# A graph network in four layers: three sums of tiles, and one chunk's norms and mean, at other places in the order of steps

## The chip, the cores and the metric

The kernel runs on one core of a Trainium2 chip. The time is device microseconds of one execution, as the median of three runs. Its engines are TensorE (PE in the profile), VectorE (DVE), ScalarE (ACT), GpSimd (POOL) and SyncE (SP, which issues the DMAs here). Each works through its own queue in order; between them semaphores tell that a step is done.

## The reference

`x` is (8, 2048, 64), `adj` a sparse (2048, 2048) matrix whose rows sum to one. Four layers follow each other, each `x = layernorm(x + L(x, adj))`:

```python
# L0: per-node weights from an embedding of 16, terms 1, A, 2AA-1 of x
w = jnp.einsum('nd,dkio->nkio', embedding, weight)
out = jnp.einsum('bnki,nkio->bno', x_g, w) + b
# L1: attention over edges above 0.5, then elu
# L2: agg = (adj + 1) @ (x W^T + b) / degree
# L3: three steps of effects = adj @ v; h = relu([v, effects] W1 + b1); v = h W2 + b2
```

With these inputs every row of `adj` has two or more entries, so none is above 0.5, and the kernel computes L1 as one mean over all nodes, and checks by flags that it may (a slow general path stands behind a branch and isn't taken).

## The kernel before

The 512 columns (8 batches of 64) are four chunks `c` of 128; the 2048 nodes are 16 tiles of 128, grouped in four quarters `j`. All engines run through the same lists of steps: `HEAD` (lines 87 to 95), `MIDDLE` from `middle_order()` (line 98 on) and `TAIL` from `last_order()`. A step is a tuple, and each engine does its own part of it, in the order of the list. So a list is the order of every engine's queue.

`MIDDLE` holds layer 0's 64 rounds, `Z` with `add`: round 4u + t, with unit u = 4c + j, is one tile of one chunk. PE multiplies the tile's three terms with the 16 embedding weights: two halves g of 18 matmuls each, into three pairs of PSUM banks in turn. VectorE adds five of the eight results of each half into `X` and `Y`, ScalarE copies three scaled into `AT`, and GpSimd (`add`) sums these into `AC` and then all into `X`: five operations, one of 384 columns and four of 128. ScalarE's part of a round waits (`s_ab`) until GpSimd's first operation of the round before has read `AT`; PE's half waits (`s_za`) until ScalarE has read the half three before it.

Ahead of a round's `Z` stand a quarter or two of the products for later units (`P2`, `P1`, bank 0, evicted by `E2`, `E1`: high half on ScalarE, low half on VectorE), and in units with c < 3 and j < 2, so in rounds 0 to 7, 16 to 23 and 32 to 39, a term: `dx` or `t1` in bank 1, evicted by ScalarE, VectorE and, for `t1`, GpSimd (a split into high and low half).

`at(g, steps)` puts steps behind round g. `xs` k (`dve_xs`, `pool_xs`) takes the sums of tiles 2k and 2k+1 over the 64 channels on VectorE, and subtracts the mean and adds the bias on GpSimd, with four operations of 512 columns. A round of chunk 0 needs this for its tile (`s_xc`), and `E1 12` needs it for tiles 0 to 7, `E1 14` and `scales 1` for all 16. `scales` are small steps on VectorE, one on ScalarE.

The norm of layer L and chunk c is `sq` (square, ScalarE) and `red` (sum, VectorE) for each quarter, `var` (VectorE, with a root on ScalarE), `rs` (five small VectorE steps) and an `apply` for each quarter (VectorE). Behind layer 0's norm stand `sum` (three adds on GpSimd), `mean` (PE), `row_a` and `row_b` (VectorE, with an exp on ScalarE) and `addrow` for each quarter (GpSimd); behind layer 1's the `split` for each quarter: high half on ScalarE, low half and a bias add (`bc`) on GpSimd. `bt` are 64 GpSimd steps that build combined masks for later; `chk` is a count on ScalarE. For chunk c these begin at round 16(c+1) + 3: chunk 0 in rounds 19 to 37, chunk 1 in 35 to 53, chunk 2 in 51 to 69; chunk 3 has an order of its own behind round 63. What is put at rounds 64 and later stands in `TAIL`, among the products `P` of layer 2 (evicted by `E`), the steps `W` and `D`, and the checks `ovr` and `sgn`.

Of the kernel before, what the change touches and what calls it, by code (L numbers as in the profile page):

```python
# [58 lines left out]
def pieces(kind, n):  # L59
    return [(kind, n, q) for q in range(4)]  # L60
# [22 lines left out]
def place(p, c, j):  # L83
# [7 lines left out]
        + pieces("P1", 0) + [("E1", 4), ("E1", 5), ("wm",), ("E1", 6), ("E1", 7), ("E1", 8)]  # L91
        + pieces("P1", 1) + [("nb",), ("wn",), ("E1", 9), ("dx", 0), ("t1", 0), ("dx", 1), ("t1", 1), ("dx", 2)]
        + [("xs", 0)]
        + pieces("P1", 2) + [("t1", 2), ("dx", 3), ("t1", 3), ("xs", 1), ("E1", 10), ("bounds",), ("xs", 2)]
        + pieces("P1", 3)[0:3] + pieces("P2", 0) + [("E2", 0), ("P1", 3, 3), ("E1", 11)])


def middle_order():

    after, rest = {}, {}

    def at(g, *steps):

        (after if g < 64 else rest).setdefault(g if g < 64 else g - 64, []).extend(steps)

    for c in range(NC):
        g = 16 * c
        for j in range(4):  # L110
            late = (c, j) == (3, 3)
            at(g + 4 * j + (4 if late else 6), ("sq", 0, c, j))
            at(g + 4 * j + (4 if late else 7), ("red", 0, c, j))
        g += 16
        if c < 3:
            at(g + 3, ("var", 0, c))
            at(g + 4, ("rs", 0, c), ("apply", 0, c, 0))
            for j in (1, 2, 3):
                at(g + 4 + j, ("apply", 0, c, j))
            at(g + 7, ("sum", c))  # L120

            g += 9
            at(g, ("mean", c), ("row_a", c))
            at(g + 1, ("row_b", c))
            for j in range(4):
                at(g + 2 + j, ("addrow", c, j))
                at(g + 4 + j, ("sq", 1, c, j))
                at(g + 5 + j, ("red", 1, c, j))
            at(g + 8, ("var", 1, c))
            for j in range(4):  # L130
                at(g + 9 + j, *[("rs", 1, c)][j:], ("apply", 1, c, j), ("split", c, j))
        else:
            at(g, ("var", 0, c), ("rs", 0, c), *[("apply", 0, c, j) for j in range(4)], ("sum", c))
            at(g + 5, ("mean", c), ("row_a", c), ("row_b", c))
            for j in range(4):
                at(g + 6, ("addrow", c, j))
            for j in range(4):
                at(g + 6 + j // 2 / 2, ("sq", 1, c, j))
                at(g + 6.5 + j // 2 / 2, ("red", 1, c, j))
            at(g + 7, ("var", 1, c))  # L140
            for j in range(4):
                at(g + 8 + j, *[("rs", 1, c)][j:], ("apply", 1, c, j), ("split", c, j))

        for k in range(4):
            at(16 * c + 9 + 2 * k, ("chk", 4 * c + k))
    for k in range(5):
        at(2 * k + 1, ("xs", 3 + k))
    at(9, ("scales", 0))
    at(11, ("scales", 1))
    at(13, ("scales", 2))  # L150
    at(15, ("scales", 3))
    for k, g in enumerate((18, 24, 27, 29)):
        at(g, ("scales", 4 + k))

    free = [2, 4, 6, 8] + [g for g in range(10, 64) if g not in (23, 39, 55) and g % 16 not in (2, 3, 4, 5)]
    free = sorted(free + [g for g in (18, 19, 20, 21, 56, 57, 58, 60, 61, 62)][:48 - len(free)])
    for i in range(48):
        at(free[i], ("bt", i))
    order = []
    for u in range(16):  # L160
        c, j = divmod(u, 4)
        beside = []
        if u in (1, 2, 5, 6):
            v = {1: 4, 2: 5, 5: 6, 6: 7}[u]
            beside += pieces("P1", v) + [("E1", 8 + v)]
        beside += pieces("P2", u + 1) + [("E2", u + 1)] if u < 15 else pieces("P", 0) + [("E", 0)]
        each = len([x for x in beside if x[0][0] == "P"]) // 4
        for t in range(4):
            n = 0
            while beside and (n < each or beside[0][0][0] == "E"):  # L170
                n += beside[0][0][0] == "P"
                order.append(beside.pop(0))
            order += [("Z", u, t), ("add", u, t)]
            order += after.pop(4 * u + t, [])
            if c < 3 and j < 2:
                v = 4 * (c + 1) + 2 * j + t // 2
                order.append(("dx" if t % 2 == 0 else "t1", v))
    return order, rest
# [119 lines left out]
def cut(n, jj, what):  # L298
    return "cut", n, jj, what

MIDDLE, _rest = middle_order()
TAIL = last_order(_rest)
_cut = TAIL.index(("branch",))
# [1969 lines left out]
```

How the kernel before makes its waits and increments, by code:

```python
    def __call__(self, ins):  # L42
        ins.then_inc(self.sem, 1)
        self.n += 1
        self.e.wait_ge(self.sem, self.n)
# [669 lines left out]
        def sync_head(e):  # L715
# [4 lines left out]
            def pair(m):  # L720
                if m >= RING:
                    e.wait_ge(s_bm, 2 * (m - RING) + 2)
                h, t = divmod(2 * m, NT)
                e.dma_start(landing[m % RING].rearrange("p (t i) -> p t i", t=2),
                            atr[:, h, t:t + 2, :]).then_inc(s_ring[m % RING], 16)
# [11 lines left out]
            e.dma_start(SM[:, :], sm_in).then_inc(s_small, 16)  # L738
            e.dma_start(BX, bx_in.rearrange("p (k n) -> p k n", n=128)).then_inc(s_bx, 16)
            tiles_of_x(4)
            pair(4)
            pair(5)
            for h in range(2):
                e.dma_start(T3[64 * h:64 * h + D, 0:1024 + C], embt_in[D * h:D * h + D, :]).then_inc(s_embed, 16)
            tiles_of_x(5)
            for m in range(6, NT):
                pair(m)
            e.wait_ge(s_zp, 8 * NT)
            for it in range(NT):
                if it:
                    e.wait_ge(s_sign, it)
                e.dma_start(rowt, ar[it]).then_inc(s_land, 16)
# [1 line left out]
        def sync_fast(e):  # L754
            for u, (c, j) in enumerate(x[1:] for x in TAIL if x[0] == "out"):
                e.wait_ge(s_n[3], u + 1)
                e.dma_start(orr[:, c, 4 * j:4 * j + 4, :], xpart(c, j)).then_inc(s_out, 16)
            e.wait_ge(s_out, 16 * 16)
# [2 lines left out]
        def pe_aux(e, step):  # L761
            e.wait_ge(*aux_free[step])
            return bank(aux_bank[step])
```

## Time and profile before

| | us |
|---|---|
| median of 3 runs | 1032.59 (1032.51 to 1033.38) |
| profiled execution | 1033.26 |
| its span | 1031.5 |
| PE busy | 1008.9 |
| DVE busy | 678.2 |
| POOL busy | 555.2 |
| ACT busy | 456.5 |

The span goes from the first instruction to the last; about 1.8 us lie around it. The granted TensorE clock was 0.996 of full speed on the mean. The 64 rounds lie between 108.13 and 525.22 us. Times within the trace count from the start of the span. A mark in square brackets behind a row tells how long the engine was idle before it and who ended that; a row without one followed its engine's previous work directly, or nearly so.

### The profile page before, as it was taken

The numbers are of one execution on the slowest core, as the hardware profiler recorded it, in microseconds if no ns is written. First come the engines' busy times: TensorE is split into PE (matmuls) and PEld (weight loads), VectorE is DVE, ScalarE is ACT, GpSimd is POOL, SyncE is SP. The second block draws the span as 40 slices with busy tenths as digits, with TensorE's granted clock in tenths as the row PEclk, the third lists the DMA queues.
The fourth block names the chain that finished last, engine by engine and source line by source line (L and its number), as shares of the span: only waits on it lengthen the run. The fifth ranks groups of instructions, "written<-read, shape, count | busy, mean of one in ns | idle before, by whom it ended". The sixth has DMA issues, their size and how long they took to land.

```text
span 1031.5 us, 18649 instructions
## 1 busy us (share of the span) xinstructions
PE 1008.9 (98%) x6854; PEld 485.1 (47%) x6854; DVE 678.2 (66%) x1683; ACT 456.5 (44%) x1109; POOL 555.2 (54%) x645
## 2 busy tenths in 40 slices
PE   7999999999999999999999999999999999999995
PEld 3445444444444444434445556555555545455552
DVE  3886565656577796577667767786763546657556
ACT  4632233453345545543552554342556555232632
POOL 0004498666558698879878465474534243323311
PEclk9999999999999999999999999999999999999998
DMA  9930000000000000000010111000032231000022
GB/s 367 403 141 1 1 2 2 1 2 1 1 1 2 1 2 2 1 2 1 1 42 1 41 42 42 2 1 1 2 123 98 107 123 42 3 2 21 21 62 62
DMA packets 14658, 45.65 MB, mean 44 GB/s; under 512 B 960, under 2 KB 9280, under 8 KB 10080
## 3 DMA queue, kind: packets, MB, share of 16 engines
q1 hardware_dynamic: 14560, 44.39, 11.8%
q8 instruction: 56, 0.92, 0.4%
q14 instruction: 42, 0.34, 0.1%
HBM read 40.19 MB, written 4.19 MB: 43 GB/s over the span
## 4 chain that ended last, share of the span: by engine, by line
PE 83%; DVE 9%; ACT 3%; DMA 2%; issue 1%; POOL 0%; SPq 0%; ACTq 0%; DVEq 0%; POOLq 0%
PE PS L961 28%; PE PS L924 23%; PE PS L794 21%; DMA BW<-at_in 2%; PE PS L779 2%; PE PS L781 2%; PE PS L780 2%; DVE BW L1227 1%; DVE T L1230 1%; ACT WZ L1074 1%; DVE X L1230 1%; DVE X L1542 1%; PE PS L788 1%; PE PS L787 1%; PE PS L786 1%
## 5 line engine op out<-in xcount | busy, mean ns | idle before, releaser
L794 PE MATMUL PS<-BW,S 128*128 128x512 fp8e4 x1280 | 290.9, 379 | 1.2 <-DVE R L1230 0.7
L1074 ACT ACTIVATE T<-PS,SM 128x128 f32<-128x128 f32 x384 | 113.1, 366 | 208.5 <-DVE X L1230 127.3
L924 PE MATMUL PS<-WZ,R 64*128 64x512 f16 x1536 | 198.0, 377 | 1.7 <-ACT T L1074 1.7
L794 PEld LDWEIGHTS PS<-BW,S 128*128 128x128 f16 x1280 | 120.2, 98 | 150.1 <-issue 17.0
L961 PE MATMUL PS<-BW,S 128*128 128x512 fp8e4 x768 | 173.1, 379 | 0.0
L1748 POOL TENSOR_TENSOR T<-T 128x128 f32<-128x128 f32 (+1 forms) x192 | 125.0, 651 | 73.0 <-ACT T L1074 62.9
L1230 DVE SCALAR_TENSOR_TENSOR X<-PS,SM,X 128x128 f32<-128x128 f32 x320 | 109.6, 342 | 77.8 <-PE PS L924 76.9
L924 PEld LDWEIGHTS PS<-WZ,R 64*128 64x128 f16 x1536 | 69.5, 94 | 104.6 <-issue 26.3
L961 PEld LDWEIGHTS PS<-BW,S 128*128 128x128 f16 x768 | 73.8, 98 | 83.3 <-issue 0.5
L961 PE MATMUL PS<-BW,T 128*128 128x512 fp8e4 x480 | 109.3, 379 | 0.0
L1748 POOL TENSOR_TENSOR S<-R,S 128x512 f16<-128x512 f32 (+1 forms) x46 | 52.7, 1153 | 102.4 <-ACT S L1074 102.4
L1230 DVE SCALAR_TENSOR_TENSOR T<-PS,SM,T 128x128 f32<-128x128 f32 x256 | 87.8, 343 | 27.5 <-PE PS L924 27.5
L924 PE MATMUL PS<-WZ,T 64*128 64x512 f16 x768 | 103.8, 376 | 0.0
L1748 POOL TENSOR_TENSOR T<-R,T 128x512 f16<-128x512 f32 x40 | 50.6, 1273 | 85.0 <-ACT T L1074 51.3
L1074 ACT ACTIVATE WZ<-WZ,ra 128x2048 f16<-128x2048 f32 (+1 forms) x32 | 63.8, 1994 | 41.2 <-DMA WZ<-a_in 41.2
L1230 DVE SCALAR_TENSOR_TENSOR R<-PS,cs,R 128x512 f32<-128x512 f32 x48 | 35.9, 749 | 65.7 <-PE PS L788 29.0
L1772 POOL TENSOR_TENSOR BW<-BW 128x512 fp8e4<-128x512 fp8e4 x64 | 70.8, 1112 | 2.7
L961 PEld LDWEIGHTS PS<-BW,T 128*128 128x128 f16 x480 | 46.3, 98 | 52.9
L1230 DVE SCALAR_TENSOR_TENSOR R<-PS,ra,R 128x128 f32<-128x128 f32 x176 | 48.6, 341 | 31.0 <-PE PS L781 17.8
L1748 POOL TENSOR_TENSOR X<-X,T 128x128 f32<-128x128 f32 x128 | 59.3, 463 | 10.0
L779 PE MATMUL PS<-hat,T 128*128 128x128 f16 x320 | 57.2, 219 | 3.4 <-DVE T L1230 2.5
L846 PE MATMUL PS<-BW,S 128*128 128x512 fp8e4 x240 | 53.6, 386 | 6.1 <-DVE BW L1227 6.1
(210 smaller groups left out, 1494.6 us busy)
## 6 DMA issues: line engine op xcount, KB each, us to landing
WZ<-a_in SPq DMA_DIRECT2D x16, 1024.0 KB, 4.8
BW<-at_in SPq DMA_DIRECT2D x8, 1024.0 KB, 19.1
R<-at_in SPq DMA_DIRECT2D x7, 1024.0 KB, 13.8
out<-X SPq DMA_DIRECT2D x16, 256.0 KB, 2.3
X<-x_in SPq DMA_DIRECT2D x3, 1024.0 KB, 21.1
T<-w_in SPq DMA_DIRECT2D x1, 1536.0 KB, 16.6
R<-at_in SPq DMA_DIRECT2D x2, 512.0 KB, 4.5
SM<-sm_in SPq DMA_DIRECT2D x1, 520.5 KB, 19.2
```

The lines of the kernel that those rows point to most:

```text
L779: e.matmul(ok, th, hat[:, 0, kind, :], start=True, stop=False)
L780: e.matmul(ok, tl, hat[:, 0, kind, :], start=False, stop=False)
L781: m = e.matmul(ok, th, hat[:, 1, kind, :], start=False, stop=True)
L786: e.matmul(o, hat[:, 0, kd, :], T[:, c, 0, block(j)], start=alone, stop=False, skip_group_check=on)
L794: m = e.matmul(o, stile(h, t, c), Bm[:, t, block(j)], start=(t == 0 and h == 0), stop=(last and t == NT - 1 and h == 1))
L846: e.matmul(bank(2 * c + j), stile(h, jt, c), Bm[:, jt, block(j)], start=(jt == 0 and h == 0), stop=False)
L924: m = e.matmul(bank(b0 + q), halves[kd][zh][r, :], WZ[r, wh, kd, block(g)], start=(i == 0), stop=(i == 8))
L961: m = e.matmul(o, half_of(n, what, h, q % 2)[:, t, :], b[:, 4 * (q % 2) + t, :], start=(s in (0, 1, 3) and q % 2 == 0 and t == 0 and h == ...
L1074: return e.activation(o, i, f, **kw)
L1230: return e.scalar_tensor_tensor(out=o, in0=a, scalar=s, in1=b, op0=f, op1=g)
L1748: return e.tensor_tensor(o, a, b, f)
L1772: e.tensor_tensor(o, a, b, f, saturate=False).then_inc(s_bt, 1)
```

## The change

Three things move; no step is added or removed. `xs 2` goes from the end of the head to behind round 1, and `xs 3` to `xs 7` two rounds further on each, to rounds 3 to 11. `scales 0` to `scales 4` follow by two rounds. And for chunk 1 everything that is counted from `g` (the norm of layer 0, `sum`, `mean`, the row steps, the norm of layer 1, the splits) goes six rounds further on: to rounds 41 to 59 in place of 35 to 53. The squares and sums of layer 0's own norm stay where they are, as do the `bt` and `chk` steps.

```diff
--- before.py
+++ after.py
@@ -91,7 +91,7 @@
         + pieces("P1", 0) + [("E1", 4), ("E1", 5), ("wm",), ("E1", 6), ("E1", 7), ("E1", 8)]
         + pieces("P1", 1) + [("nb",), ("wn",), ("E1", 9), ("dx", 0), ("t1", 0), ("dx", 1), ("t1", 1), ("dx", 2)]
         + [("xs", 0)]
-        + pieces("P1", 2) + [("t1", 2), ("dx", 3), ("t1", 3), ("xs", 1), ("E1", 10), ("bounds",), ("xs", 2)]
+        + pieces("P1", 2) + [("t1", 2), ("dx", 3), ("t1", 3), ("xs", 1), ("E1", 10), ("bounds",)]
         + pieces("P1", 3)[0:3] + pieces("P2", 0) + [("E2", 0), ("P1", 3, 3), ("E1", 11)])
 
 
@@ -111,7 +111,8 @@
             late = (c, j) == (3, 3)
             at(g + 4 * j + (4 if late else 6), ("sq", 0, c, j))
             at(g + 4 * j + (4 if late else 7), ("red", 0, c, j))
-        g += 16
+
+        g += 22 if c == 1 else 16
         if c < 3:
             at(g + 3, ("var", 0, c))
             at(g + 4, ("rs", 0, c), ("apply", 0, c, 0))
@@ -143,13 +144,14 @@
 
         for k in range(4):
             at(16 * c + 9 + 2 * k, ("chk", 4 * c + k))
-    for k in range(5):
-        at(2 * k + 1, ("xs", 3 + k))
-    at(9, ("scales", 0))
-    at(11, ("scales", 1))
-    at(13, ("scales", 2))
-    at(15, ("scales", 3))
-    for k, g in enumerate((18, 24, 27, 29)):
+
+    for k in range(6):
+        at(2 * k + 1, ("xs", 2 + k))
+    at(11, ("scales", 0))
+    at(13, ("scales", 1))
+    at(15, ("scales", 2))
+    at(17, ("scales", 3))
+    for k, g in enumerate((20, 24, 27, 29)):
         at(g, ("scales", 4 + k))
 
     free = [2, 4, 6, 8] + [g for g in range(10, 64) if g not in (23, 39, 55) and g % 16 not in (2, 3, 4, 5)]
```

## Rows read from the trace of the kernel before

**Rows 1.** The page, section 1: busy us (share of the span), xinstructions of each engine.
```profile
PE 1008.9 (98%) x6854; PEld 485.1 (47%) x6854; DVE 678.2 (66%) x1683; ACT 456.5 (44%) x1109; POOL 555.2 (54%) x645
```

**Rows 2.** Waits: engine, line it waits at <- who ended it: us in total, times, longest.
```profile
PE PS L924 <- ACT T L1074: 1.7, 1, 1.7
...
PE PS L832 <- DVE R L1230: 1.6, 2, 1.3
```

**Rows 3.** Timeline of PE, 113 to 130: start us, us, engine, line, out<-in [idle before].
```profile
114.40 0.82 PE L924 MATMUL PS<-WZ,R 64*128 64x512 f16 x6
...
120.67 0.82 PE L924 MATMUL PS<-WZ,R 64*128 64x512 f16 x6
...
124.47 0.82 PE L924 MATMUL PS<-WZ,R 64*128 64x512 f16 x6 [1.69 <-ACT T L1074]
...
128.80 0.82 PE L924 MATMUL PS<-WZ,R 64*128 64x512 f16 x6
```

**Rows 4.** Timeline of POOL, 104 to 126.
```profile
117.83 1.03 POOL L1720 TENSOR_TENSOR X<-X,hat 128x512 f32<-128x512 f32 x1 [7.38 <-issue]
...
122.51 2.06 POOL L1748 TENSOR_TENSOR T<-T 128x384 f32<-128x384 f32 x3
```

**Rows 5.** Timeline of PE, 350 to 379.
```profile
363.90 0.82 PE L924 MATMUL PS<-WZ,R 64*128 64x512 f16 x6
...
369.28 0.23 PE L832 MATMUL PS<-i,T 128*128 128x128 f16 x1 [1.32 <-DVE R L1230]
...
371.56 0.82 PE L924 MATMUL PS<-WZ,R 64*128 64x512 f16 x6
```

**Rows 6.** Timeline of DVE, 362 to 369 and 447 to 460.
```profile
364.60 0.88 DVE L1529 TENSOR_TENSOR T<-T 128x32 f32<-128x32 f32 x1
...
449.06 0.19 DVE L1529 TENSOR_TENSOR T<-T 128x32 f32<-128x32 f32 x1
...
456.32 0.68 DVE L1542 TENSOR_TENSOR X<-X,T 128x512 f32<-128x512 f32 x1
```

**Rows 7.** Timeline of PE, 447 to 468.
```profile
449.11 0.82 PE L924 MATMUL PS<-WZ,R 64*128 64x512 f16 x6
...
455.71 0.82 PE L924 MATMUL PS<-WZ,R 64*128 64x512 f16 x6
...
461.53 0.82 PE L924 MATMUL PS<-WZ,R 64*128 64x512 f16 x6
```

**Rows 8.** Groups by form, POOL, 453.3 to 477: xcount, busy us, mean ns, idle us before.
```profile
L1748 POOL TENSOR_TENSOR X<-X,bc 128x512 f32<-128x512 f32 x4 | 5.8, 1440 | 0.3
L1748 POOL TENSOR_TENSOR S<-X,S 128x512 f16<-128x512 f32 x4 | 4.6, 1156 | 0.3
L1748 POOL TENSOR_TENSOR T<-T 128x384 f32<-128x384 f32 x4 | 4.4, 1110 | 1.6 <-ACT T L1074 1.6
L1748 POOL TENSOR_TENSOR T<-T 128x128 f32<-128x128 f32 x6 | 3.3, 556 | 0.5
```

**Rows 9.** Groups by form, POOL, 482.9 to 530.86.
```profile
L1748 POOL TENSOR_TENSOR T<-T 128x384 f32<-128x384 f32 x8 | 8.0, 998 | 3.1 <-ACT T L1074 3.1
...
L1748 POOL TENSOR_TENSOR T<-T 128x128 f32<-128x128 f32 x17 | 7.7, 455 | 1.3
...
L1748 POOL TENSOR_TENSOR X<-X,ROW 128x512 f32<-128x512 f32 x4 | 5.1, 1270 | 0.3
```

**Rows 10.** Timeline of POOL, 440 to 490.
```profile
446.14 0.99 POOL L1748 TENSOR_TENSOR X<-X,T 128x128 f32<-128x128 f32 x2
...
483.45 0.99 POOL L1748 TENSOR_TENSOR X<-X,T 128x128 f32<-128x128 f32 x2
```

**Rows 11.** Timeline of ACT, 518 to 612, and of PE, 600 to 612.
```profile
530.88 0.63 ACT L1074 ACTIVATE R<-X 128x512 f32<-128x512 f32 x1 [0.32 <-POOL X L1748]
...
548.09 0.60 ACT L1074 ACTIVATE T<-PS 128x512 f16<-128x512 f32 x1 [1.12 <-PE PS L944]
...
608.46 0.23 PE L779 MATMUL PS<-hat,T 128*128 128x128 f16 x1 [0.87 <-DVE X L1230]
```

## The prediction

> **What bounds the kernel now.** I read the page first: TensorE is busy 98% of the span [rows 1]. So a change of order can win only where TensorE stands, or lose where it makes TensorE stand. The waits of PE come next. The longest inside the rounds are [rows 2]: one of 1.7 us for ScalarE, and two, 1.6 us together, for a term's low half on VectorE. I count rounds from 0 to 63 (the steps `Z`). The starts of the rounds on PE give the price of each stall, since a round between stalls takes the same time whenever it holds the same matmuls.
>
> Rounds 1 and 2 hold the same kind of work, but round 1 takes 120.67 - 114.40 = 6.27 us and round 2 takes 128.80 - 120.67 = 8.13 us [rows 3]: 1.86 us lost. In the middle of round 2 PE waits for ScalarE [rows 3]. ScalarE was late because it may not overwrite `AT` before GpSimd's first add of round 0, and GpSimd began that add only at 122.51, when the four operations of `xs 2`, begun at 117.83, were through [rows 4]: 4.68 us of queue.
>
> Round 37 takes 371.56 - 363.90 = 7.66 us, 1.39 us over 6.27, and PE waits there for VectorE's low half of `dx 14` [rows 5]. Ahead of it VectorE had `rs` and `apply` of layer 0, chunk 1. A small step of such an `rs` took 0.88 us there, against 0.19 elsewhere [rows 6].
>
> Round 51 takes 6.60 us where the next takes 5.82 [rows 7]: 0.78 us. PE wanted the bank of product `P2 13`, whose low half stood on VectorE behind `rs` and `apply` of layer 1, chunk 1. After round 63 PE stands next at 608.46, for 0.87 us [rows 11], and then hardly before the end.
>
> **The change, part by part.** No instruction is added or removed; only places in the queues change.
>
> Part 1, `xs 2` behind round 1 and the later sums one turn later. GpSimd's first add of round 0 comes to stand at 117.83 in place of 122.51 [rows 4], 4.68 us earlier. That is more than the 1.86 us by which PE was held, so the stall goes: -1.86 us. What is late next is the data: round 4 needs `xs 2`, and ScalarE's `E1 12` ahead of round 5 needs tiles 0 to 7, so `xs 3`. GpSimd does adds 0 and 1, `xs 2`, a split of `t1`, add 2, `bt 0`, add 3 and then `xs 3`. With four adds of some 3.2 us (a first operation of 1.0 and four of 0.46 by [rows 9], with the gaps between them), two `xs` of 4.68 and two steps of about 1.2 us (as the splits of [rows 8]) that is 117.83 + 24.6 = 142.4, if it never waits. PE, freed of its stall, begins round 3 at 120.67 + 6.27 = 126.9 and ends the product of `E1 12` two rounds later, at 139.5 at the earliest. So the eviction may come up to 2.9 us late; but PE asks for its bank only behind the terms of round 5, and I cost it at nothing. The moved `scales` steps are small VectorE steps in rounds that have no stall: nothing.
>
> Part 2, chunk 1's layer-0 norm from rounds 35 to 38 into rounds 41 to 44. `rs` and `apply` leave the queue ahead of `dx 14`. Even unblocked (five steps at the 0.19 us and an apply at the 0.68 of [rows 6]) they are 1.6 us, more than 1.39: -1.39 us. In rounds 41 to 44 no `dx` or `t1` follows. `E2 11` follows `rs` there, as `E2 13` did in round 51, but without a `split` on ScalarE between them; so its high half is done while VectorE still works on the norm, and I cost this at nothing. The wait of 0.3 us at round 35 (chunk 0's norm, the smaller of the two of [rows 2]) is untouched.
>
> Part 3, chunk 1's layer-1 norm and its splits from rounds 50 to 53 into rounds 56 to 59. The stall at round 51 goes: -0.78 us. Sum of the three: -4.03 us.
>
> What it costs lies on GpSimd. The four splits and the bias adds behind them took 4.6 + 5.8 = 10.4 us [rows 8]. They now stand between rounds 56 and 59, where GpSimd also has chunk 2's sum, the `bt` steps and the adds. The room there is little: from the end of add 55 to that of add 63 GpSimd waited 3.1 us in all [rows 9]. There is one credit: GpSimd was then still paying for the splits. Add 55 ended at 484.44, 11.27 us behind the start of its round (461.53 + 2 x 5.82), while a settled one, add 49, ended at 447.13, 9.66 us behind its own (449.11 - 2 x 5.82) [rows 7, 10]. With the splits gone from ahead of it, add 55 is settled: 1.6 us. VectorE's norms slow GpSimd's adds besides. In the stretch of the splits a first add took 1110 ns [rows 8] against 998, and the small ones 556 against 455 [rows 9]: 4 x 0.11 + 6 x 0.10, and as much as the latter again for the second pair, 1.7 us. That stretch held the norms of both chunks; half of it moves, 0.8 us. So the last add of round 63 ends 10.4 + 0.8 - 3.1 - 1.6 = 6.5 us later than now, measured against a PE that never waits.
>
> Who waits for that? ScalarE's square of chunk 3's last quarter starts on that very add [rows 11], and behind it in order stand the reduce, `var`, root, `rs`, four applies, `rs` of chunk 2 and the evictions of the products `P`. The first place where this string has room is 548.09: ScalarE had idled 1.12 us for PE [rows 11]. The chain of waits goes from there through VectorE, ScalarE and GpSimd without a piece of PE until 608.46, where PE waits [rows 11]. So of the 6.5 us PE pays 6.5 - 1.1 = 5.4. A part of it (1 to 2.5 us) will be paid near rounds 61 and 62, where ScalarE waits for GpSimd's add as in round 2; the rest at the latest near 608. Both are the same debt and are not added.
>
> Sum: -4.03 + 5.4 = +1.4 us. The profiled execution was 1033.26 us (span 1031.5) and gives 1034.7; the median of the runs, 0.67 us lower, gives 1034.0 us. Bounds: with no slowdown at all (a bias add at the 1.27 us that [rows 9] has for the same shape: 9.7 for 10.4) the debt is 3.9 and the result 1032.5. With the whole 1.7 us and 0.5 us for VectorE's small steps, it is +2.7: 1035.3.
>
> A rule is to be weighed here. The slowdown of [rows 8] is 0.1 us on most operations, and 0.88 for 0.19 us on VectorE's side [rows 6]. The Trainium skill, "SBUF — State Buffer", section "Who interferes with whom", says that a VectorE instruction with two SBUF inputs and a GpSimd one that reads SBUF exclude each other for the whole instruction. By that rule four applies of 0.68 us each would hold GpSimd for up to 2.8 us in place of my 0.8, and the sum would be +3.4; the rows of GpSimd show less.
>
> **The rivals.**
>
> A. The debt is not passed on: rows 61 to 63 or the string behind them have room that I don't see, and only the gain is left. It gives 1032.59 - 4.03 = 1028.6 us; half of it passed on gives about 1031.3. For it: GpSimd is only 54% busy overall [rows 1], and a new order may fill waits that I counted once. Against it: the last square starts on the add with no room, and the chain behind it shows no PE.
>
> B. Slower. GpSimd and VectorE, both now without pauses in rounds 56 to 59, hold each other up operation by operation. If the four moved applies and the five steps of `rs` cost GpSimd their full length (4 x 0.7 and a little), the debt is 8.4 and the time 1032.59 - 4.03 + 7.4 = 1036.0 us. It decides once the slowdown is above about 1.5 us in place of 0.8; then the result is over the bound of 0.2%.
>
> C. Part 1 doesn't do what it says: `xs 3` comes late for `E1 12`, or the wait only shifts by a round. Then 1.86 us stay: 1035.9 us.
>
> **How the numbers follow.** 0.2% of 1032.6 is 2.1 us, about what a measurement of this kernel can tell from no change: below 1030.5 is faster, above 1034.7 slower. Forecast (debt passed on, 1032.5 to 1035.3, likeliest 1034.0): 0.50, of which 0.14 is above 1034.7. A: 0.32, of which 0.24 is below 1030.5 and 0.08 between. B: 0.13, C: 0.05, both slower. So faster 0.24, within 0.2% 0.44, slower 0.32. The range has to take in A's full gain below and B above, since to leave either out would leave out too much: 1028.6 to 1036.0. The forecast's own range is 1032.5 to 1035.3.
>
> **What would show it.** In the changed kernel's waits of PE the 1.7 us for ScalarE near 124 and the two of 1.3 and 0.7 us near 369 and 454 should be gone; round 2 should take 6.27, rounds 37 and 51 6.27 and 5.82. New: GpSimd without an idle mark from round 56 to 63, a wait of PE for ScalarE near round 61 or 62, and the wait at the end of the chain, 0.87 us now, grown by some 3 us. If that wait is still 0.9 us and no new one stands near round 62, A is right. If GpSimd's adds in rounds 57 to 60 take over 4 us each, B is. I am wrong altogether if PE waits in rounds 42 to 45 for `E2 11` behind the moved norm.

## The result and the profile after

The changed kernel took 1035.1 us (median, 1034.6 to 1036.0) against 1032.9 us (1031.7 to 1034.4) for the kernel before in the same sessions. The ratio is 1.0022, with a 95% interval of 1.0015 to 1.0029. It is slower by 2.2 us: 1.1 us more than the 1034.0 I gave, inside the forecast's own range (1032.5 to 1035.3) near its upper end. The ratio is just over the 0.2% that I had set between "no change" and "slower", and its interval holds that bound.

The page of the changed kernel, section 1 (engine, busy us, share of the span), under its span of 1033.8 us; [rows 1] answer to it:

```profile
PE 1010.2 (98%) x6854; PEld 485.4 (47%) x6854; DVE 675.4 (65%) x1683; ACT 456.3 (44%) x1109; POOL 553.5 (54%) x645
```

It tells nothing: PE is 98% busy in both, and the number of instructions is the same. The waits of PE between 110 and 615 us do tell it (line it waits at <- who ended it: us in total, times, longest). The code behind the change has moved down by two lines, so L926 is what L924 was:

```profile
PE PS L926 <- ACT T L1076: 3.1, 3, 1.9
PE PS L781 <- DVE X L1232: 1.7, 1, 1.7
...
PE PS L834 <- DVE R L1232: 0.3, 1, 0.3
```

Of [rows 2] only the 0.3 us at L834 is left; the other waits are new or grown. They stand in two places. PE's timeline, 495 to 525 and 595 to 612 us (start, us, what, idle before in brackets): the lines with an idle mark, and between them the starts of rounds 60, 61, 62 and 63:

```profile
499.09 0.82 PE L926 MATMUL PS<-WZ,R 64*128 64x512 f16 x6
...
501.63 0.82 PE L926 MATMUL PS<-WZ,R 64*128 64x512 f16 x6 [0.42 <-ACT T L1076]
...
505.51 0.82 PE L926 MATMUL PS<-WZ,R 64*128 64x512 f16 x6
...
508.34 0.82 PE L926 MATMUL PS<-WZ,R 64*128 64x512 f16 x6 [0.71 <-ACT T L1076]
...
512.22 0.82 PE L926 MATMUL PS<-WZ,R 64*128 64x512 f16 x6
...
516.27 0.82 PE L926 MATMUL PS<-WZ,R 64*128 64x512 f16 x6 [1.93 <-ACT T L1076]
...
520.60 0.82 PE L926 MATMUL PS<-WZ,R 64*128 64x512 f16 x6
...
598.57 0.22 PE L781 MATMUL PS<-hat,T 128*128 128x128 f16 x1 [1.36 <-issue]
...
603.64 0.22 PE L771 MATMUL PS<-dg,S 128*128 128x128 f16 x1 [0.34 <-POOL S L1750]
...
610.71 0.23 PE L781 MATMUL PS<-hat,T 128*128 128x128 f16 x1 [1.67 <-DVE X L1232]
```

The first three waits lie in rounds 60, 61 and 62. These rounds take 6.42, 6.71 and 8.38 us, which is 0.60, 0.89 and 2.11 more than the 5.82 of an ordinary round and the 6.27 that round 62 took before (it holds a few matmuls more), 3.60 us in all. The last three waits answer to the single 0.87 of [rows 11]: 3.37 us by their marks, 2.50 more. By the starts it is 2.8 us: from the start of round 63 to the last of these waits it now takes 610.71 - 520.60 = 90.11 us, against 608.46 - 521.16 = 87.30 before. The marks show less because neighbouring rows of PE overlap: a row of six matmuls lasts 0.81 us, but the next one starts 0.65 us behind its start when nothing holds it. The overlap of 0.16 is gone wherever PE waits, and the mark counts only from the end of the row before. So PE pays 3.6 + 2.8 = 6.4 us.

And what was gained. PE's timeline, 113 to 130 us, the starts of rounds 1 to 3, then 360 to 372, the starts of rounds 37 and 38, then 443 to 458, those of rounds 51 and 52:

```profile
114.28 0.82 PE L926 MATMUL PS<-WZ,R 64*128 64x512 f16 x6
...
120.55 0.82 PE L926 MATMUL PS<-WZ,R 64*128 64x512 f16 x6
...
126.82 0.82 PE L926 MATMUL PS<-WZ,R 64*128 64x512 f16 x6
...
361.92 0.82 PE L926 MATMUL PS<-WZ,R 64*128 64x512 f16 x6
...
368.19 0.82 PE L926 MATMUL PS<-WZ,R 64*128 64x512 f16 x6
...
445.73 0.82 PE L926 MATMUL PS<-WZ,R 64*128 64x512 f16 x6
...
451.56 0.82 PE L926 MATMUL PS<-WZ,R 64*128 64x512 f16 x6
```

Rounds 1 and 2 take 6.27 us each, round 37 takes 368.19 - 361.92 = 6.27 and round 51 takes 451.56 - 445.73 = 5.83: all three stalls are gone, 1.86 + 1.39 + 0.78 = 4.03 us, as [rows 3, 5, 7] had them. 6.4 - 4.0 = +2.4 us; round 0 began 0.12 us earlier than in the trace of before, which leaves 2.3. That is what the last of the waits has moved by (610.71 against 608.46), and what the span grew by (1033.8 - 1031.5). The median grew by 2.2.

The debt itself, on GpSimd's timeline, 515 to 535 us, the add of round 63:

```profile
532.89 0.98 POOL L1750 TENSOR_TENSOR X<-X,T 128x128 f32<-128x128 f32 x2
```

No row of GpSimd carries an idle mark from 477.9 us to here. The last add ends at 533.87, where before it ended at 530.85 (the square of [rows 11] begins 0.03 us behind that). It is 3.0 us later although 4.03 us of stalls ahead of it are gone and round 0 began 0.12 us earlier: 7.2 us of debt against a PE that never waits. I had said 6.5. Of these 7.2 us PE pays 6.4, so 0.8 are absorbed on the way, where I had said 1.1.

### The profile page after: what moved, and what is told of

It reads as the page before. It is cut to its first block, busy times and chain, and to the rows that moved or that the text cites. A ratio compares the mean times of both kernels' runs of the same rounds, so it can differ in the third digit from the quotient of the medians.

```text
span 1033.8 us, 18652 instructions
## 1 busy us (share of the span) xinstructions
PE 1010.2 (98%) x6854; PEld 485.4 (47%) x6854; DVE 675.4 (65%) x1683; ACT 456.3 (44%) x1109; POOL 553.5 (54%) x645
## 4 chain that ended last, share of the span: by engine, by line
PE 85%; DVE 6%; POOL 4%; ACT 3%; issue 2%; DMA 0%; POOLq 0%; SPq 0%; ACTq 0%; DVEq 0%
PE PS L963 28%; PE PS L926 22%; PE PS L796 19%; PE PS L848 5%; PE PS L781 2%; POOL X L1750 1%; PE PS L783 1%; PE PS L782 1%; DVE X L1544 1%; POOL T L1750 1%; ACT WZ L1076 1%; PE PS L790 1%; PE PS L789 1%; PE PS L788 1%; DVE X L1232 1%
## 5 line engine op out<-in xcount | busy, mean ns | idle before, releaser
L926 PE MATMUL PS<-WZ,R 64*128 64x512 f16 x1536 | 198.3, 377 | 3.1 <-ACT T L1076 3.1
L926 PEld LDWEIGHTS PS<-WZ,R 64*128 64x128 f16 x1536 | 69.3, 94 | 106.5 <-issue 26.3
L1750 POOL TENSOR_TENSOR S<-R,S 128x512 f16<-128x512 f32 (+1 forms) x46 | 52.9, 1157 | 102.3 <-ACT S L1076 102.3
L926 PE MATMUL PS<-WZ,T 64*128 64x512 f16 x768 | 103.8, 376 | 0.0
```

What stands on the lines that cost most here:

```text
L926: m = e.matmul(bank(b0 + q), halves[kd][zh][r, :], WZ[r, wh, kd, block(g)], start=(i == 0), stop=(i == 8))
L1750: return e.tensor_tensor(o, a, b, f)
```

## The experiments

All ratios are to the kernel before, run on the same chip beside them.

### Each part alone

Part 1 alone, on the kernel before (`scales` two rounds later too, as in the change):

```diff
-        ... ("xs", 1), ("E1", 10), ("bounds",), ("xs", 2)]
+        ... ("xs", 1), ("E1", 10), ("bounds",)]
-    for k in range(5):
-        at(2 * k + 1, ("xs", 3 + k))
+    for k in range(6):
+        at(2 * k + 1, ("xs", 2 + k))
```

> The kernel before with part 1 alone: xs 2 behind round 1, xs 3 to xs 7 and scales 0 to 4 two rounds on; chunk 1 stays where it was. Theory: the wait of PE for ScalarE near 124 us (1.7) goes and nothing comes in its place, the rest of the trace is that of before moved up; span 1.9 us shorter, ratio about 0.9982. Rival (the sum of the tiles comes late and the stall only moves): ratio 1.000, with a wait of PE or of VectorE for GpSimd's X between rounds 3 and 6.

Measured: 1031.21 us, ratio 0.9984 (0.9975 to 0.9993). The waits of PE, 110 to 615 us:

```profile
PE PS L832 <- DVE R L1230: 1.6, 2, 1.3
PE PS L779 <- DVE X L1230: 0.9, 1, 0.9
PE PS L794 <- DVE R L1230: 0.7, 1, 0.7
```

The wait for ScalarE is gone and nothing has come in its place: part 1 is a gain by itself, 1.8 us of the 1.86. Rival C is out.

Parts 2 and 3 alone:

```diff
-        g += 16
+        g += 22 if c == 1 else 16
```

> The kernel before with parts 2 and 3 alone: chunk 1's norms, mean and splits six rounds on; xs and scales stay where they were. Theory: the stalls at rounds 37 and 51 go (-2.2 us), GpSimd's debt is that of the changed kernel and costs some 6.2 us, so +4 us, ratio about 1.004; the wait for ScalarE near 124 us is there, and new ones of some 3.5 us stand at rounds 60 to 62. Rival (the loss of the changed kernel comes from part 1, or from both together): ratio near 1.000 or below.

Measured: 1037.15 us, ratio 1.0041 (1.0027 to 1.0055). The waits of PE, 110 to 615 us:

```profile
PE PS L924 <- ACT T L1074: 4.9, 4, 1.9
...
```

Behind it stand 1.7, 1.4, 0.3 and 0.3. These are the waits of the changed kernel, one by one, with the wait of 1.75 us at round 2 besides, since part 1 is missing here. So the whole loss comes from the moved norm. By the starts it costs 6.4 us and brings 1.39 + 0.78 = 2.2, so +4.2; measured are +4.1. The change is the sum of a part that gains and one that loses.

### A late last add: is GpSimd's lateness handed on?

```diff
+                    if n4 == 63:
+                        for _ in range(5):
+                            pc(add(AC, AC, AC))
```

> The kernel before, where GpSimd does five more operations of 384 columns (each an addition of AC to itself, overwritten at once) ahead of the add of round 63: some 5.3 us more on its queue, of which 0.7 us lies in an idle time; nothing waits for it but the add. It measures what a late last add costs. Theory: the add ends 4.6 us later, the first 1.1 us are covered at ScalarE's eviction near 548, the rest (3.5 us) comes out in PE's waits between 596 and 610 us: ratio about 1.0034. Rival A (the string behind round 63 has room for it): ratio 1.000.

Measured: 1035.79 us, ratio 1.0026 (1.0016 to 1.0037). The kernel before has nothing else changed here. The last add ends at 534.20, 3.35 us later than before, and the rounds ahead of it lie 0.36 us earlier in this trace (the add of round 62 begins at 521.07, before at 521.43): it is 3.7 us late. PE's timeline, 590 to 612 us:

```profile
598.83 0.22 PE L779 MATMUL PS<-hat,T 128*128 128x128 f16 x1 [1.41 <-issue]
...
610.96 0.23 PE L779 MATMUL PS<-hat,T 128*128 128x128 f16 x1 [1.66 <-DVE X L1230]
```

With 0.34 us at 603.90 the three waits are those of the changed kernel to within 0.05 us. The last of them ends 610.96 - 608.46 = 2.50 us later than before, and with the 0.36 us by which the rounds lie earlier 2.9 of the 3.7 us are handed on and 0.8 are absorbed, as in the changed kernel. Most of it is absorbed where [rows 11] show the slack of 1.12 us: in the changed kernel ScalarE's row of 530.88 comes 3.0 us later, its row of 550.13 comes 2.0 us later. Between there and 560.54 the lateness grows again, to 2.2 us; what gives back these 0.2 us I didn't settle. I had expected 4.6 us of lateness and not 3.7. The 0.74 us that GpSimd waited ahead of this add were already taken off in that number; the five operations were shorter than I took them for: the eight rows of 384 and 128 columns take 6.58 us where three took 2.07, so some 0.9 us each and not 1.06.

Rival A falls with this run: the chain has no further room. The same shows across the runs. Wherever the last add comes late, PE's last wait ends 76.8 us behind the end of that add: 76.84 us in the changed kernel, 76.76 here, and 76.79 to 76.80 in the run with four masks moved and in the three runs on the apply below. What makes the last add later makes the whole kernel later.

### The masks out of the way: is it the fullness of GpSimd's queue?

Four `bt` of rounds 56 to 59 (one of the two at round 56 stays) and the one of round 45, put at rounds 39 and 50 to 53:

```diff
-    free = ... if g not in (23, 39, 55) and g % 16 not in (2, 3, 4, 5)]
+    free = ... if g not in (23, 45, 55, 56, 57, 58, 59) and (g % 16 not in (2, 3, 4, 5) or g in (50, 51, 52, 53))]
```

> The changed kernel with only the four mask steps of GpSimd (bt) at rounds 56 to 59 taken out and put at rounds 39 and 50 to 52 instead; the other later ones stay, none goes behind round 63. Theory of the debt on GpSimd (in the changed kernel PE pays some 6 us of GpSimd's lateness: 3.6 at rounds 60 to 62 and 2.5 near 609): a bt takes about 1.1 to 1.2 us, so four of them take 4.4 to 4.8 us off the queue; PE gets back 4 us of the 6.1 (the slack ahead of 548 us takes the rest), so about 1031.0 us where the kernel before has 1032.9, a ratio near 0.998. Rival 1 (the masks only fill what would be waiting time, so that moving them is worth nothing): 1035, 1.002. Rival 2 (the earlier rounds have no room for them and PE waits there instead): 1033 to 1035, with new waits of PE between 435 and 470 us.

Measured: 1030.94 us, ratio 0.9978 (0.9968 to 0.9988), 4.2 us below the changed kernel. The waits of PE for ScalarE at L926 are gone; what is left is 0.3 us at round 35, 0.5 us for VectorE in round 59 and 0.2 + 0.3 + 1.7 from 593 to 605.

The `bt` of rounds 60 to 63 out as well, on top of the last edit, and put behind round 63. Of rounds 56 to 63 only round 56 still has one, not none as the expectation says:

```diff
-    for i in range(48):
+    for i in range(44):
...
-    for i in range(48, 64):
-        at(i - 46, ("bt", i))
+    for i in range(44, 64):
+        at(i - 42, ("bt", i))
```

> The changed kernel, with no bt step between rounds 56 and 63: four go to rounds 39 and 50 to 53, where chunk 1's steps stood, four behind round 63. GpSimd's queue is 8.7 us shorter from round 56 to 63. Theory (the loss is GpSimd's debt of 7.2 us): the debt is gone, PE waits neither at rounds 60 to 62 nor more than 0.9 us near 608, and the whole gain is left: about 4 us below before, ratio 0.996. Rival (the loss is VectorE's, whose norms of chunk 1 and chunk 2 now meet between rounds 52 and 59): ratio near 1.002 as with the change.

Measured: 1030.2 us, ratio 0.9974 (0.9964 to 0.9984). GpSimd again waits for ScalarE ahead of the last add (0.57 us), so its debt is paid by then, also with the one mask at round 56. The time is only 0.7 us better than with four moved, since a wait of 1.62 us near 605 stayed. The next run has no mask from round 55 to 63 and none more behind round 63 than the kernel before. It puts a second one at rounds 42, 43, 44, 48 and 53 (the loops over 48 and 16 masks are again those of the changed kernel):

```diff
+    free = sorted([g for g in free if g < 56] + [18, 19, 20, 21, 42, 43, 44, 53, 48])
```

> The changed kernel with all mask steps of GpSimd out of rounds 55 to 63, as in the run that took them out before, but the surplus stands at earlier rounds (a second one at 42, 43, 44, 48 and 53) and none behind round 63. In the run with four of them behind round 63 PE still waited 1.62 us at 605.6 where the kernel before has 0.87. Theory 1 (these four stood ahead of chunk 3's norms and were paid there): the wait goes back to 0.9 us, the waits of rounds 60 to 62 stay away, one of about 0.5 us in round 59 stays: about 1029.4 against 1032.9, a ratio near 0.9965. Theory 2 (the 0.75 us come from elsewhere in the moved norm, from VectorE's queue): 1030.2, 0.9974, with the wait near 605 at 1.6 us again. If the rounds 42 to 53 have no room, PE waits there for ScalarE behind GpSimd: over 1031.

Measured: 1029.17 us, ratio 0.9958 (0.9944 to 0.9971). The wait near 605 is 1.04 us: 0.58 of the 0.75 us too much are gone. I put this down to the four masks behind round 63. The one of round 56 moved too, but GpSimd's idle time ahead of the last add had covered that one. The last run moves chunk 2's `row_b` one round on as well:

```diff
-            at(g + 1, ("row_b", c))
+            at(g + (2 if c == 2 else 1), ("row_b", c))
```

> As the run with all masks out of rounds 55 to 63 and the surplus at earlier rounds, and besides chunk 2's row_b (VectorE, ahead of its layer-1 norm) one round later, behind round 59 in place of 58. In round 59 PE waited 0.53 us for the bank of E2 15, whose low half stood on VectorE behind that row_b and an apply of chunk 1. Theory (that low half was late because of this queue): with row_b behind it the wait goes, round 59 takes 5.9 us, and the time is 0.5 us below the other run: about 1028.9, a ratio near 0.996. Rival (the apply alone makes it late, or chunk 2's norms, pushed back a round, come late for something behind round 63): no gain, or the wait at the chain's end near 605 grows by as much.

Measured: 1028.62 us, ratio 0.9953 (0.9940 to 0.9967). All waits of PE between 110 and 615 us:

```profile
PE PS L781 <- DVE X L1232: 0.9, 1, 0.9
PE PS L834 <- DVE R L1232: 0.3, 1, 0.3
```

The debt is gone and the 4.03 us are left: 4.2 us below the kernel before. The wait for the low half in round 59 went with `row_b`; the difference in time between these last two runs, 0.5 us, is no more than their intervals, and only the row of the wait shows that it is gone. So the same move of the norm is a gain where GpSimd's queue has room for it, and this version beats both kernels.

### What an apply costs GpSimd

Three runs change only the four applies of layer 1, chunk 1 (rounds 57 to 60 on VectorE). First on 8 columns in place of 512:

```diff
+                    if (L, c) == (1, 1):
+                        v, r = v[:, :, :, 0:1], r.unsqueeze(3)
+                        e.tensor_tensor(v, v, r, ALU.mult).then_inc(s_n[L], 1)
+                        continue
```

> The changed kernel with the four applies of layer 1's norm of chunk 1 (on VectorE, rounds 57 to 60, some 0.7 us each) done on one channel of 64 alone, so all but one channel of that normalization is left out; every step, wait and place stays. It asks what VectorE's applies cost GpSimd. Theory (they share the memory's ports for a part, a few tenths of a us on an operation): the two splits and adds beside them get 0.2 to 0.3 us shorter each, PE gets back 0.5 to 1.2 us: about 1034.2, a ratio near 1.001 against 1.0022 of the changed kernel. Rival (each holds the other for its whole length): 4 x 0.7 = 2.8 us come back, about 1032.3, a ratio below 1.0. Rival 2 (no effect of the applies at all; the small steps of rs and the sums are what slows GpSimd): same 1.0022.

Measured: 1033.32 us, ratio 1.0001 (0.9992 to 1.0010), 1.8 us less than the changed kernel by the medians: more than the theory's 0.5 to 1.2, less than the rival's 2.8. Since the intervals are some 1 us wide on either side, the trace is the surer measure: from the end of add 55 to that of the last add GpSimd takes 53.02 us, against 54.96 in the changed kernel, 1.9 us less. This is where my small slowdown fell. Then a reduce over the same 512 columns, with one operand in SBUF, of the same length:

```diff
+                    if (L, c) == (1, 1):
+                        red(e, r, v, ALU.max).then_inc(s_n[L], 1)
+                        continue
```

> The changed kernel with each of the four applies of layer 1's norm of chunk 1 (VectorE, two operands in SBUF, 512 columns, 0.68 us) replaced by a maximum over the channels of the same 512 columns: one operand in SBUF, about the same length on VectorE. The normalization of that chunk is left out so. With the applies shrunk to 8 columns, GpSimd's operations beside them got 2.1 us shorter in sum and the time fell from 1035.1 to 1033.3. This run tells what does it. Theory (it is the apply's second SBUF operand: each of the two engines waits for the other's whole instruction): the reduces hold up nobody; GpSimd's first operations of rounds 57 to 59 take 2.1 us for three in place of 2.6 to 2.9, and the time is that of the small applies, about 1033.2, a ratio of 1.000. Rival (any VectorE instruction of that length slows GpSimd, whatever its operands): as the changed kernel, 1035.1, 1.002.

Measured: 1033.27 us, ratio 1.0005 (0.9996 to 1.0014). The rows show why. The changed kernel, GpSimd's timeline and VectorE's, 478 to 503 us (the rows of rounds 57 to 59 that bear on it):

```profile
482.96 2.61 POOL L1750 TENSOR_TENSOR T<-T 128x384 f32<-128x384 f32 x3
...
486.71 1.15 POOL L1750 TENSOR_TENSOR S<-X,S 128x512 f16<-128x512 f32 x1
487.94 1.59 POOL L1750 TENSOR_TENSOR X<-X,bc 128x512 f32<-128x512 f32 x1
...
491.61 2.89 POOL L1750 TENSOR_TENSOR T<-T 128x384 f32<-128x384 f32 x3
...
495.64 1.16 POOL L1750 TENSOR_TENSOR S<-X,S 128x512 f16<-128x512 f32 x1
...
499.15 2.56 POOL L1750 TENSOR_TENSOR T<-T 128x384 f32<-128x384 f32 x3
...
481.90 1.13 DVE L1225 TENSOR_SCALAR T<-T 128x32 f32<-128x32 f32 x1
483.07 0.93 DVE L1538 TENSOR_TENSOR T<-T 128x32 f32<-128x32 f32 x1
484.03 0.69 DVE L1544 TENSOR_TENSOR X<-X,T 128x512 f32<-128x512 f32 x1
...
487.23 1.19 DVE L1544 TENSOR_TENSOR X<-X,T 128x512 f32<-128x512 f32 x1
...
495.92 0.69 DVE L1232 SCALAR_TENSOR_TENSOR R<-PS,R 128x512 f16<-128x512 f32 x1 [0.28 <-ACT R L1056]
```

With the reduces, the same stretch and engines:

```profile
482.75 2.06 POOL L1753 TENSOR_TENSOR T<-T 128x384 f32<-128x384 f32 x3
...
487.19 1.27 POOL L1753 TENSOR_TENSOR X<-X,bc 128x512 f32<-128x512 f32 x1
...
490.52 2.07 POOL L1753 TENSOR_TENSOR T<-T 128x384 f32<-128x384 f32 x3
...
497.42 2.06 POOL L1753 TENSOR_TENSOR T<-T 128x384 f32<-128x384 f32 x3
...
483.82 0.69 DVE L1235 TENSOR_REDUCE T<-X 128x8 f32<-128x512 f32 x1
...
487.01 0.67 DVE L1235 TENSOR_REDUCE T<-X 128x8 f32<-128x512 f32 x1
```

The first three operations of an add take 2.06 us together, and with an apply beside them 2.61, 2.89 and 2.56; the bias add takes 1.59 in place of 1.27. Together 0.55 + 0.82 + 0.50 + 0.32 = 2.2 us. About 0.2 of them are not the applies': with the reduces, and with the small applies too, the last two operations of the same add take 1.15 us in place of 0.99, beside a small step of VectorE that here falls into the 2.89. So four applies cost 2.0 us, and from the end of add 55 to that of the last add the run with the reduces takes 53.02 us, 1.9 us less than the changed kernel.

The reduces are as long as the applies (0.69, 0.67), the first two lie beside the same operations of GpSimd, and these take their usual 2.06 and 1.27. So it is not VectorE being busy. A reduce differs from an apply in two things, though: it has one operand in SBUF where the apply has two, and it writes 8 columns where the apply writes 512. The row at 495.92 speaks against the writing: 0.69 us, 512 columns written, with one input from PSUM and one from SBUF, beside a split of GpSimd that takes its usual 1.16. So it is the second operand in SBUF, and each apply holds GpSimd for 0.3 to 0.7 us, up to its whole length of 0.68. The apply at 487.23 shows the other side: it began under the split, which ended at 487.86, and took 1.19 us; I read it as having waited for that end. This agrees with the Trainium skill, "SBUF — State Buffer", "Who interferes with whom": a VectorE instruction with two SBUF inputs and a GpSimd one that reads SBUF exclude each other for the whole instruction, and a `tensor_reduce` never contends on this chip.

The third doubles the request:

```diff
+                    if (L, c) == (1, 1):
+                        fc(e.tensor_tensor(v, v, v, ALU.max))
```

> The changed kernel with one more VectorE instruction ahead of each of these four applies: a maximum of the quarter with itself, 512 columns, both operands in SBUF, 0.68 us, which changes no value. It doubles what a two-operand instruction asks of the port beside a GpSimd queue that never idles. Theory (exclusion for the whole instruction, and GpSimd's lateness is handed on to PE one for one): 4 x 0.5 to 0.7 us more on GpSimd's operations, so 2.0 to 2.8 us more of PE's waits, about 1037.4, a ratio of 1.0042 to 1.005. Rival (the slowdown is a sharing that spreads thin, or the first apply's 0.5 us were an accident of where it fell): under 1 us more, 1.0022 to 1.003. It also adds 4 x 0.7 us on VectorE; if PE then waits for a low half on VectorE near rounds 57 to 60 (as it did for 0.5 us at round 59 with the masks out), that part is no work of the port and is to be read off apart.

Measured: 1036.71 us, ratio 1.0035 (1.0022 to 1.0049), 1.6 us more than the changed kernel, under the 2.0 to 2.8 of the theory. GpSimd's timeline from 489 us to the last add, a row of VectorE, and one of PE:

```profile
489.48 3.05 POOL L1776 TENSOR_TENSOR BW<-BW 128x512 fp8e4<-128x512 fp8e4 x2
...
507.32 2.51 POOL L1752 TENSOR_TENSOR T<-T 128x384 f32<-128x384 f32 x3
...
534.30 0.98 POOL L1752 TENSOR_TENSOR X<-X,T 128x128 f32<-128x128 f32 x2
...
497.42 1.64 DVE L1546 TENSOR_TENSOR X<-X,T 128x512 f32<-128x512 f32 x1
...
502.42 3.31 PE L796 MATMUL PS<-BW,S 128*128 128x512 fp8e4 x8 [3.67 <-DVE R L1232]
```

Two mask steps together grew from 2.15 to 3.05 us, two single ones from 1.09 to 1.54 and 1.55, and further operations by 0.2 to 0.45 each; the last pair of applies comes only at 504.87, so the add at 507.32 is still slowed (2.51 for 2.06). From the end of add 55 to that of the last add GpSimd takes 56.16 us, 1.2 more than the changed kernel's 54.96 and 3.1 more than with no applies of that size. The last add ends at 535.28, 1.4 us later than in the changed kernel (0.2 of it lay ahead of this stretch already); PE's last wait ends at 612.08, also 1.4 us later. So the longer time is GpSimd's lateness, handed on one for one, as the theory had it.

What the theory had wrong is the size: the second request cost GpSimd 1.2 us and not 2.0 to 2.8. The rest fell on VectorE: its eight instructions of 0.68 us took from 0.83 to 1.64. Its queue then ran late, and PE stood 3.67 us in round 59 for a low half. But this wait is no further loss. In its place the three waits of rounds 60 to 62 are gone but for one of 1.02 us in round 59, and so are those of 1.36 and 0.34 us near 598 and 603. PE's waits between 110 and 615 us come to 6.7 us in this run and to 6.8 in the changed kernel. The run doesn't show that the loss grows in proportion; it shows that between two queues that are both full the cost can fall on either.

## Why the prediction was right, and where it was off

The gains. Parts 1 to 3 give 1.86, 1.39 and 0.78 us, each to within 0.02 us. No wait of PE came from `xs 3` at its new place, nor from `E2 11` in rounds 42 to 45: both costed at nothing, rightly. The 0.3 us at round 35 stayed.

The sign and the mechanism. The debt on GpSimd is there, is handed on almost whole, and shows where I said: GpSimd without an idle mark, PE waiting for ScalarE in rounds 60 to 62, and the rest from 598 to 611. The late add settles that this is cause and not company, and the mask runs that it is the fullness of GpSimd's queue. I had the part near rounds 61 and 62 at 1 to 2.5 us (it is 3.6) and the growth at the chain's end at some 3 (it is 2.8); the sum counts.

The size. I had +1.4 us, and by the starts it is +2.4. Two terms were off. The debt is 7.2 us where I had 6.5, and the slack is 0.8 where I had 1.1. In the debt the mis-sized term is the slowdown of GpSimd by VectorE, which I took at 0.8 us. The splits and bias adds without any apply beside them take 4 x 1157 + 4 x 1269 ns = 9.7 us (the means in the run with the reduces), and VectorE's holds cost 2.2, so 11.9 us, where I had 10.4 + 0.8 = 11.2. The 10.4 of [rows 8] held 0.7 of slowdown already, so on top of it 1.5 us were due. Two smaller slips cancel. The credit for a settled add 55 was 1.4 us and not 1.6: it ended 9.9 us behind the start of its round. And some 0.2 us of the operations that [rows 9] count were slowed before and are not now. The range held because its upper end had the whole 1.7 us and 0.5 more. Of the 1.1 us between 1034.0 and the measured 1035.1, 0.3 are no fault of the sum: the kernel before itself took 1032.9 us in these sessions, where I had 1032.6.

The step that is off is the halving. The total that I read from the means was right: 1.7 us and the 0.7 in the bias adds, 2.4 in all, against 2.3 when the same stretch is added up operation by operation. Two of the four adds in it show what the means hid (kernel before, GpSimd's timeline):

```profile
463.47 2.66 POOL L1748 TENSOR_TENSOR T<-T 128x384 f32<-128x384 f32 x3
...
470.08 2.52 POOL L1748 TENSOR_TENSOR T<-T 128x384 f32<-128x384 f32 x3
```

The first operations of the other two took 2.07. So single groups lose 0.3 to 0.6 us and their neighbours nothing, and the loss goes by the applies that meet a working GpSimd, not by the time or the number of norms. In that stretch GpSimd was idle for 1.60 us ahead of 457.46, and chunk 1's apply of 456.32 fell into it and cost nothing. In the full queue of rounds 57 to 60 all four of them counted. Halving the sum because two norms stood there had no ground.

Rival B had the mechanism, with a price of 2.8 us for the applies where 2.0 was measured, and set it on top of the 10.4 that held some of it, and so 1036.0 us. It was to decide above a slowdown of about 1.5 us, and that is where it lies. The sign that I gave for it, adds of over 4 us each in rounds 57 to 60, did not show (the longest of them took 3.95 us, where a settled one takes 3.1); it was set too high to find a hold of 0.3 to 0.7 us.

## What to carry to other kernels

To move work off a stalled spot into a later one, add up the queue of each engine that the moved steps use, to the next idle time of that engine; what doesn't fit there is a debt, and it has to be followed along who waits for whom until it meets idle time or the critical engine. Move the filler (here the masks, which are due much later) ahead of the gap together with the work, and the same move becomes a gain. Where a GpSimd queue is full, count each VectorE instruction with two SBUF operands beside it by itself, here at 0.3 to 0.7 us for one of 0.68, and not by a mean over the stretch.

## What the runs showed of the hardware

I hadn't expected that an instruction of VectorE slows GpSimd by 0.3 to 0.7 us or by nothing, at the same length to 0.02 us: the apply, with two operands in SBUF, does and the reduce doesn't. The hold works from both sides. A VectorE step of 32 columns and 0.19 us took 0.93 us beside GpSimd's add (483.07 in the changed kernel, the same with the reduces), and an apply of 0.68 up to 1.64. VectorE can also be held where it has a single tensor input: the `TENSOR_SCALAR` at 481.90 took 1.13 us beside GpSimd's sums, where the same step took 0.18 in the kernel before at 449.51, while GpSimd was idle. So a single tensor input doesn't keep every VectorE step clear of GpSimd; whether such a step also slows GpSimd these rows don't show.

In the run with two applies PE stood for 3.67 us in round 59, and the clock fell behind it. Windows of that run (window, us, busy us (count) of PE, PEld, DVE, ACT, POOL, granted clock, DMA share, GB/s):

```profile
500.00:504.00 4.00, 1.58 (x5) 0.67 (x6) 3.86 (x13) 1.05 (x3) 3.61 (x7) 0.84 0.00 0
504.00:508.00 4.00, 4.00 (x25) 1.34 (x24) 3.97 (x7) 1.50 (x7) 3.92 (x4) 0.73 0.00 0
508.00:520.00 12.00, 12.00 (x96) 4.90 (x92) 6.25 (x23) 7.44 (x17) 11.14 (x15) 1.00 0.01 1
```

The mean clock was 0.84 and 0.73 of the full 2.4 GHz in two stretches of 4 us, a mix of its two levels, and full again behind them. The eight matmuls at 502.42 show the price: 3.31 us, where the same eight take 1.90 in the other rounds, 1.4 us more; the row behind them lost another 0.2. In this run the slow stretch cost nothing in the end, since PE then waited less for the chain behind GpSimd's last add (1.67 us of waiting were still left at 612.08). After the wait of 1.93 us in the changed kernel the clock did not fall; its window 514 to 522 us:

```profile
514.00:522.00 8.00, 6.07 (x52) 2.72 (x50) 3.36 (x11) 5.25 (x14) 7.37 (x12) 1.00 0.00 0
```

So the stalls of this change cost little more than themselves. On a PE with no later wait to hide it, a slow stretch such as the one behind the 3.67 us would add some 1.6 us by these rows; that is an estimate, and no run here shows the case.
